# Four graph layers on one core: semaphores cleared inside stages, block-only preparations moved, two reloads split and one request moved

## The chip, the cores and the metric

The kernel runs on one core of a Trainium2 chip. The metric is the device time of one execution in microseconds (us); the median of three executions of the kernel before is 4069.77 us (4069.27 to 4072.3).

## The reference

A graph has 3125 nodes with 256 features and 50000 edges (`src`, `dst`, sorted by `dst`). Four layers follow one another, each added to its input and normalised over the features:

```python
# layer 0: one weight matrix per edge type (20), edges weighted
msg = h_all[edge_src, rel_type] * norm;  relu(segment_sum(msg, edge_dst))
# layer 1
relu(x @ W + segment_sum((x @ M)[edge_src], edge_dst))
# layer 2: attention with 4 heads, 4 node types, 8 edge types
k, q, v = _typed_matmul(h, ..., node_type)            # a matrix per node type
score = sum((q @ relation_att)[etype, col] * k[row]) * pri[etype] / 8
alpha = softmax of score over the edges of a target node
agg = segment_sum(alpha * (v @ relation_msg)[etype, row], col)
out = sigmoid(skip)[node_type] * _typed_matmul(agg, a_linears, node_type)
# layer 3: two graph convolutions
x = relu(segment_sum(norm * (x @ W[l])[src], dst) + b[l] + x_res @ resW + resb)
```

## The kernel before, in words

Nodes are held as 25 tiles of 128 rows (`NT`). The edges are sorted on the chip and held as 391 tiles of 128 edges (`USED`; 196 pairs). The program is a row of stages, each an `nc.Block()` with one instruction stream per engine; at a block's end all five engines meet in a barrier before the next block starts. In order:

1. `constants`, and `sort_and_relation_table` (L221 to L508): TensorE multiplies the nodes with the 20 matrices of layer 0 while VectorE sorts the edges and GpSimd (POOL) scatters the edges' records, 8 numbers each, to HBM (`records`, L313).
2. `reload_records` (L519): SyncE (SP) requests all sorted records back in one transfer (L529), clears the semaphores of the stages before (L530), VectorE and ScalarE turn two fields of every record into integer row numbers (`rows_i`, L540 and L546).
3. `aggregate_edges` for layer 0 (called `rel`), `first_layer_nodes` (L1696), `aggregate_edges` for layer 1 (`conv_edges`).
4. A block in which SP does nothing but clear spent semaphores (L2380).
5. `attention_tables` (L1835): the nodes are normalised, scattered by node type to `sorted_x` (L1902), read back in five parts of five tiles (L1889), multiplied by type, and the products scattered to `table8k`, `table8v` and `q_rows` (L1909, L1914). When all of these have landed, SP requests `q` back (L1895).
6. `attention_edges` (L1462): `attention_scores`, then `attention_sum`, in one block.
7. A second block that only clears (L2390), and a block in which VectorE adds two bias rows (L2399).
8. `attention_output` (L2109): SP loads weights, `skip` and the node types (L2148 to L2153); ScalarE waits for the last three before anything else (L2189); VectorE makes the gates from them; TensorE multiplies.
9. `aggregate_edges` (`gcn0_edges`), a third block that only clears (L2405), `hidden_nodes` (L1761), `aggregate_edges` again, `last_nodes`.

An edge sweep (`aggregate_edges`, and each half of `attention_edges`) works so: POOL issues one indirect gather per edge tile, 391 in all, into a ring of 16 pairs of tiles (`gather_all`, L624); SP relays arrivals to the others and hands slots back (`relay_pairs`, L641); for each of 220 items TensorE multiplies one-hot matrices with a gathered pair and VectorE adds the product to the window of its target nodes (L1062). POOL first needs a slot back at its 33rd gather. There are six sweeps, so 2346 gathers. The orders are written out by hand; nothing schedules them.

In the first sweep `ItemColumns` (L680) first makes the items' columns from the records: TensorE turns the records (L697), VectorE makes `tile_key` (L727) and `pick` (L731). In the scores TensorE waits for `q_back` before its first product (L1134), and ScalarE requests spread rows on its own DMA queue (L676).

## Time and profile before

| | us |
|---|---|
| median of three executions (lowest, highest) | 4069.77 (4069.27, 4072.3) |
| the profiled execution | 4077.45 |
| its span, from the first to the last instruction | 4075.5 |

| stage | from | to |
|---|---|---|
| sort and relation table | 0 | 559.8 |
| reload of the records | 559.8 | 568.3 |
| sweep `rel` | 568.3 | 1064.2 |
| first layer's nodes | 1064.2 | 1104.7 |
| sweep `conv_edges` | 1104.7 | 1600.3 |
| block that clears | 1600.3 | 1604.4 |
| attention tables | 1604.4 | 1873.0 |
| scores and sums | 1878.8 | 2890.3 |
| two blocks: clearing, biases | 2890.3 | 2896.5 |
| attention output | 2896.5 | 3002.8 |
| sweep `gcn0_edges` | 3002.8 | 3497.6 |
| block that clears | 3497.6 | 3500.7 |
| hidden nodes | 3500.7 | 3531 |
| sweep `gcn1_edges`, last nodes | 3531 | 4075.5 |

A timeline row reads: start, duration, engine, source line, operation, written tile <- read tiles, and in brackets how long the engine had been idle before and what ended that. "PEq", "POOLq", "SPq" are the sequencers of these engines; a release by one of them at the line of a block is the barrier. "DMA a<-b" is the landing of that transfer. SPq rows of DMA show the issuing instruction, not the transfer. Clearing a semaphore leaves no row.

### The profile page before, as it was taken

The numbers are of one execution on the slowest core, as the hardware profiler recorded it, in microseconds if no ns is written. First come the engines' busy times: TensorE is split into PE (matmuls) and PEld (weight loads), VectorE is DVE, ScalarE is ACT, GpSimd is POOL, SyncE is SP. The second block draws the span as 40 slices with busy tenths as digits, with TensorE's granted clock in tenths as the row PEclk, the third lists the DMA queues.
The fourth block names the chain that finished last, engine by engine and source line by source line (L and its number), as shares of the span: only waits on it lengthen the run. The fifth ranks groups of instructions, "written<-read, shape, count | busy, mean of one in ns | idle before, by whom it ended". The sixth has DMA issues, their size and how long they took to land. (4 is left out here: it accounts for less than half of the span.)

```text
span 4075.5 us, 64605 instructions
## 1 busy us (share of the span) xinstructions
PE 3135.5 (77%) x11818; PEld 2154.4 (53%) x11818; DVE 2219.7 (54%) x7526; ACT 926.8 (23%) x2670; POOL 2753.2 (68%) x2879
## 2 busy tenths in 40 slices
PE   6999938878788775795888878888877667677777
PEld 4444426656566653343667667676434444544444
DVE  6500037666666655445888858676654344334435
ACT  2333300000200001441444456555310000200001
POOL 4777767777677776335777767777237777477773
PEclk9999968898898986898887769777887888878788
DMA  4333323333333334677555546555223333333332
GB/s 146 149 146 150 145 76 106 105 105 106 96 106 105 106 105 140 244 299 243 164 165 163 163 138 176 161 163 160 66 74 106 105 105 106 99 105 106 106 105 85
DMA packets 226899, 540.02 MB, mean 133 GB/s; under 512 B 73483, under 2 KB 107949, under 8 KB 212877
## 3 DMA queue, kind: packets, MB, share of 16 engines
q0 software_dynamic: 136528, 374.97, 31.1%
q1 hardware_dynamic: 57880, 103.46, 7.0%
q10 hardware_dynamic: 32164, 57.91, 4.7%
q8 instruction: 123, 2.02, 0.2%
q14 instruction: 204, 1.66, 0.1%
HBM read 390.04 MB, written 146.09 MB: 132 GB/s over the span
## 5 line engine op out<-in xcount | busy, mean ns | idle before, releaser
L635 POOL DMA_INDIRECT gcn_edges_g<-table,rows_i x782 | 741.9, 949 | 397.9 <-issue 186.8
L1016 PE MATMUL ps<-gcn_edges_g,gcn_edges_onehot 128*128 x1760 | 618.8, 490 | 311.3 <-SPq L651 278.1
L1062 DVE TENSOR_TENSOR acc<-acc,ps 128x256 f32 (+1 forms) x880 | 370.2, 421 | 849.3 <-PE ps L1016 835.4
L1016 PEld LDWEIGHTS ps<-gcn_edges_g,gcn_edges_onehot 128*128 128x128 f32 x1760 | 382.7, 237 | 525.9 <-issue 477.3
L313 POOL DMA_INDIRECT records<-rec,slots x391 | 381.5, 976 | 167.6 <-issue 124.5
L635 POOL DMA_INDIRECT score_g<-table8v,rows_i x391 | 379.9, 972 | 132.6 <-issue 112.8
L635 POOL DMA_INDIRECT rel_g<-table,rows_i x391 | 372.1, 952 | 132.2 <-issue 96.0
L635 POOL DMA_INDIRECT score_g<-table8k,rows_i x391 | 373.1, 954 | 128.7 <-issue 110.7
L635 POOL DMA_INDIRECT conv_edges_g<-table,rows_i x391 | 371.8, 951 | 127.4 <-issue 93.3
L365 PE MATMUL ps<-w,xt 128*128 128x512 f32 x1000 | 435.8, 595 | 18.0 <-ACT xt L335 18.0
L1141 PE MATMUL ps<-q,onehot_t 128*128 x880 | 310.5, 486 | 120.4 <-DVE onehot_t L1240 96.1
L1375 PE MATMUL ps<-vx,score_onehot 128*128 128x260 f32 x880 | 303.5, 477 | 87.0 <-ACT vx L1399 48.9
L1016 PE MATMUL ps<-conv_edges_g,conv_edges_onehot 128*128 x880 | 277.8, 445 | 103.7 <-SPq L651 96.5
L1016 PE MATMUL ps<-rel_g,rel_onehot 128*128 x880 | 276.3, 443 | 96.1 <-SPq L651 88.8
L365 PEld LDWEIGHTS ps<-w,xt 128*128 128x128 f32 x1000 | 187.9, 190 | 251.2 <-issue 227.0
L1141 PEld LDWEIGHTS ps<-q,onehot_t 128*128 128x128 f32 x880 | 188.0, 236 | 161.8 <-issue 140.5
L1399 ACT ACTIVATE vx<-score_g,vx 128x64 f32 x880 | 234.5, 336 | 104.7 <-SPq L651 72.9
L1016 PEld LDWEIGHTS ps<-conv_edges_g,conv_edges_onehot 128*128 128x128 f32 x880 | 171.1, 215 | 162.7 <-issue 143.5
L1375 PEld LDWEIGHTS ps<-vx,score_onehot 128*128 128x128 f32 x880 | 182.6, 230 | 118.8 <-issue 95.7
L1016 PEld LDWEIGHTS ps<-rel_g,rel_onehot 128*128 128x128 f32 x880 | 172.2, 217 | 136.9 <-issue 118.0
L1054 DVE TENSOR_SCALAR gcn_edges_onehot<-cols,near 128x128 f32<-128x128 f32 x880 | 223.7, 308 | 1.3 <-issue 1.1
L343 ACT ACTIVATE tb<-ps 128x512 f32<-128x512 f32 x250 | 149.3, 597 | 296.4 <-PE ps L365 296.4
(327 smaller groups left out, 4799.4 us busy)
## 6 DMA issues: line engine op xcount, KB each, us to landing
table<-tb SPq DMA_DIRECT2D x50, 1280.0 KB, 4.6
score_dst_bc<-dst_rows ACTq DMA_DIRECT2D x110, 256.0 KB, 3.5
sum_dst_bc<-dst_rows ACTq DMA_DIRECT2D x110, 256.0 KB, 3.5
gcn_edges_g<-table,rows_i POOLq DMA_INDIRECT x782, 2.8
table<-acc SPq DMA_DIRECT2D x50, 128.0 KB, 1.7
records<-rec,slots POOLq DMA_INDIRECT x391
rel_g<-table,rows_i POOLq DMA_INDIRECT x391, 2.8
conv_edges_g<-table,rows_i POOLq DMA_INDIRECT x391, 2.7
```

The costliest lines, as they stand in the source:

```text
L313: pool.indirect_dma_start(out=m.records, out_offset=bass.IndirectOffsetOnAxis(ap=slots[:, j:j + 1], axis=0), in_=rec[:, j, :], in_offset=N ...
L343: nc.scalar.activation(tb[:, g // HG, (g % HG) * 512:(g % HG + 1) * 512], bank(m, g % 6, 0, 512), ACT.Copy).then_inc(emptied, 1)
L365: mm = pe.matmul(bank(m, g % 6, 0, 512), xt[:, k, :], w20[:, k, g * 512:(g + 1) * 512], start=(k == 0), stop=(k == 1))
L635: pool.indirect_dma_start(out=m.g[:, 2 * slot_of(p) + j, 0:D], out_offset=None, in_=table, in_offset=bass.IndirectOffsetOnAxis(ap=m.rows_i ...
L1016: mm = pe.matmul(bank(m, i % BANKS, 0, width), m.onehot[:, 2 * k + j, :], window(m.g, slot + j, 0, width), start=(j == 0), stop=(j == 1))
L1054: ins = nc.vector.tensor_scalar(m.onehot[:, 2 * k + j, :], m.cols[:, :], m.near[:, c:c + 1], None, ALU.is_equal)
L1062: nc.vector.tensor_tensor(acc, acc, bank(m, i % BANKS, 0, width), ALU.add).then_inc(added, 1)
L1141: mm = pe.matmul(bank(m, i % UNROLL, j * D, (j + 1) * D), onehot_t[:, i % 2, j * P:(j + 1) * P], q, start=True, stop=True)
L1375: mm = pe.matmul(bank(m, 4 + kk, 0, ACCW), m.onehot[:, 2 * kk + j, :], vx[:, kk, j, :], start=(j == 0), stop=(j == 1))
L1399: ins = nc.scalar.activation(vx[:, kk, j, h * DK:(h + 1) * DK], window(m.g, slot + j, h * DK, (h + 1) * DK), ACT.Copy, scale=vx[:, kk, j, ...
```

## The change

Clears. `take_spent` hands a list of spent semaphores over, and the next stage's SP clears them in its own block: 59 in `attention_tables` (after its small requests, before the wait for the scatters), 74 in `attention_output` (after the weights' requests, before the stores), 27 in `hidden_nodes` (before the stores). The three blocks that only cleared are gone.

Records. They come back in two transfers: tiles 0 to 31 (`FIRST`), then the rest, on a semaphore of its own (`rest_back`). The reload's block casts the first 32 tiles' row numbers only, on VectorE. The other casts, 360 and 392 columns, are VectorE's first work in `ItemColumns.vector`, behind a wait for `rest_back`; TensorE waits for it too. POOL waits for the casts (`rows_ready`) before its 33rd gather.

`q`. It is requested as SP's first instruction of `attention_edges`, not at the end of `attention_tables`.

Sorted rows. The five parts hold 2, 4, 5, 7 and 7 tiles where they held 5 each.

Biases and gates. The two additions of bias rows are VectorE's first work in the scores. `skip` is loaded in `attention_tables`; the gates compare `m.node_mark[:, :, 1]`, which the sort made, so the node types are not loaded again, and ScalarE's wait for the three small loads is gone.

```diff
@@ the reload and the first sweep @@
+FIRST = 32
 def clear_spent(sp, m):
-    for s in m.spent:
+    clear(sp, take_spent(m))
+def take_spent(m):
+    spent, m.spent = m.spent, []
+    return spent
+def clear(sp, spent):
+    for s in spent:
         sp.sem_clear(s)
...
-            sp.dma_start(m.rec[:, 0:USED, :], m.records.rearrange("(p t) f -> p t f", p=P)).then_inc(back, 16)
+            sp.dma_start(m.rec[:, 0:FIRST, :], sorted_records[:, 0:FIRST, :]).then_inc(back, 16)
+            sp.dma_start(m.rec[:, FIRST:USED, :], sorted_records[:, FIRST:USED, :]).then_inc(m.rest_back, 16)
             clear_spent(sp, m)
...
             dve.wait_ge(back, 16)
-            nc.vector.tensor_copy(m.rows_i[:, ROWS1, :], m.rec[:, :, F_SRC])
-        @block.scalar
-        def _(act):
-            act.wait_ge(blank, 2)
-            act.wait_ge(back, 16)
-            nc.scalar.activation(m.rows_i[:, ROWS20, :], m.rec[:, :, F_ROW20], ACT.Copy)
+            nc.vector.tensor_copy(m.rows_i[:, ROWS20, 0:FIRST], m.rec[:, 0:FIRST, F_ROW20])
@@ gather_all @@
     for p in range(PAIRS):
+        if rest_ready is not None and 2 * p == FIRST:
+            pool.wait_ge(rest_ready, 1)
@@ ItemColumns.tensor @@
+        pe.wait_ge(m.rest_back, 16)
@@ ItemColumns.vector @@
+        dve.wait_ge(m.rest_back, 16)
+        nc.vector.tensor_copy(m.rows_i[:, ROWS20, FIRST:TILES], m.rec[:, FIRST:TILES, F_ROW20]).then_inc(self.rows_ready, 1)
+        nc.vector.tensor_copy(m.rows_i[:, ROWS1, :], m.rec[:, :, F_SRC])
         nc.vector.tensor_scalar(m.tile_key[:, :], m.rec[:, :, F_DST], float(P), m.rowid[:, :], ALU.mult, ALU.add)
@@ attention_edges @@
         def _(sp):
+            sp.dma_start(m.q[:, 0:NT, :], m.q_rows[0:ROWS, :].rearrange("(t p) d -> p t d", p=P)).then_inc(m.q_back, 16)
             scores[0](sp)
...
         def _(dve):
+            for k in (0, 1):
+                nc.vector.tensor_tensor(m.bias[:, k, :], m.bias[:, k, :], m.bias[:, 2, :], ALU.add)
             scores[4](dve)
@@ hidden_nodes @@
+        old = take_spent(m)
...
         def _(sp):
+            clear(sp, old)
             for t in range(NT):
                 store_rows(sp, m, t, scaled, stored)
@@ attention_tables @@
+        old = take_spent(m)
...
-        PART = NT // 5
+        PARTS = ((0, 2), (2, 6), (6, 11), (11, 18), (18, NT))
...
+            sp.dma_start(m.skip[:, :], a.skip.rearrange("(o n) -> o n", o=1).to_broadcast([P, NTYPES])).then_inc(m.skip_in, 16)
+            clear(sp, old)
             sp.wait_ge(placed, 16 * NT)
-            for part in range(5):
-                sp.dma_start(xs[:, part * PART:(part + 1) * PART, :], m.sorted_x[part * PART * P:(part + 1) * PART * P, :]
+            for part, (lo, hi) in enumerate(PARTS):
+                sp.dma_start(xs[:, lo:hi, :], m.sorted_x[lo * P:hi * P, :]
                              .rearrange("(t p) d -> p t d", p=P)).then_inc(back[part], 16)
...
-            sp.dma_start(m.q[:, 0:NT, :], m.q_rows[0:ROWS, :].rearrange("(t p) d -> p t d", p=P)).then_inc(m.q_back, 16)
             sp.wait_ge(m.bias_in, 48)
+            sp.wait_ge(m.skip_in, 16)
...
             def pick(i):
                 if i < G:
-                    if i < NT and i % PART == 0:
-                        act.wait_ge(back[i // PART], 16)
+                    for part, (lo, hi) in enumerate(PARTS):
+                        if i == lo:
+                            act.wait_ge(back[part], 16)
@@ attention_output @@
+        old = take_spent(m)
...
-            sp.dma_start(skip[:, :], a.skip.rearrange("(o n) -> o n", o=1).to_broadcast([P, NTYPES])).then_inc(small_in, 16)
-            sp.wait_ge(types_zero, 1)
-            with nc.allow_non_contiguous_dma(reason="a node per partition"):
-                sp.dma_start(types_i[:, 0:NT - 1], a.node_type[0:(NT - 1) * P].rearrange("(t p) -> p t", p=P)).then_inc(small_in, 16)
-                sp.dma_start(types_i[0:LAST, NT - 1:NT], a.node_type[(NT - 1) * P:NODES].rearrange("(p o) -> p o", o=1)).then_inc(small_in, 16)
+            clear(sp, old)
             for t in range(NT):
                 store_rows(sp, m, t, scaled, stored)
...
-            act.wait_ge(small_in, 48)
             nc.scalar.activation(gate[:, :], skip[:, :], ACT.Exp, scale=-1.0).then_inc(exp_ready, 1)
...
-                ins = nc.vector.tensor_scalar(gates[:, ty, :], types_i[:, :], float(ty), skip[:, ty:ty + 1], ALU.is_equal, ALU.mult)
+                ins = nc.vector.tensor_scalar(gates[:, ty, :], m.node_mark[:, :, 1], float(ty), skip[:, ty:ty + 1], ALU.is_equal, ALU.mult)
@@ four_graph_layers: three blocks of this form are gone, and the block of the biases @@
-        with ExitStack() as c2:
-            block = c2.enter_context(nc.Block())
-            @block.sync
-            def _(sp):
-                clear_spent(sp, m)
```

How the instructions stand. SyncE around the reload, before (L515 ISA are the clears, the branches are the block's end and the next block's start) and in the changed kernel (clears: L527 ISA):

```order
L525 UNCONDITIONAL_BRANCH
L529 DMA rec_all<-records 128x3128
L515 ISA x29
L521 UNCONDITIONAL_BRANCH
L980 UNCONDITIONAL_BRANCH
```

```order
L537 UNCONDITIONAL_BRANCH
L539 DMA rec_all<-records 128x256
L540 DMA rec_all<-records 128x2872
L527 ISA x29
L532 UNCONDITIONAL_BRANCH
L991 UNCONDITIONAL_BRANCH
```

One transfer has become two, and the clears stand behind both. VectorE in the same place of the changed kernel: the cast of the reload, the block's end, and then the casts that stand ahead of `tile_key`:

```order
L551 CAST rows_i<-rec_all 128x32
L532 UNCONDITIONAL_BRANCH
L1042 UNCONDITIONAL_BRANCH
L736 CAST rows_i<-rec_all 128x360
L737 CAST rows_i<-rec_all 128x392
L738 TENSOR_SCALAR tile_key<-rec_all,rowid 128x392
```

SyncE from the read-back of the sorted rows to the scores' first relay, before and now:

```order
L1889 DMA xs<-sorted_x 128x5x256
L1889 DMA xs<-sorted_x 128x5x256 x4
L1895 DMA q<-q_rows 128x25x256
L1839 UNCONDITIONAL_BRANCH
L1473 UNCONDITIONAL_BRANCH
L645 TENSOR_LOAD release
```

```order
L1870 DMA skip<-in_skip 128x4
L527 ISA x59
L1874 DMA xs<-sorted_x 128x2x256
L1874 DMA xs<-sorted_x 128x4x256
L1874 DMA xs<-sorted_x 128x5x256
L1874 DMA xs<-sorted_x 128x7x256 x2
L1820 UNCONDITIONAL_BRANCH
L1484 UNCONDITIONAL_BRANCH
L1486 DMA q<-q_rows 128x25x256
L652 TENSOR_LOAD release
```

The request of `q` has moved across the barrier, and 59 clears stand ahead of the read-back.

## Rows read from the trace of the kernel before

**Rows 1.** Page: busy time, share of the span and instructions of each engine

```profile
PE 3135.5 (77%) x11818; PEld 2154.4 (53%) x11818; DVE 2219.7 (54%) x7526; ACT 926.8 (23%) x2670; POOL 2753.2 (68%) x2879
```

**Rows 2.** Timeline around the reload: start us, us, engine line operation, [idle before <-releaser]

```profile
559.84 0.33 SPq L529 DMA_DIRECT2D rec_all<-records  x1
566.38 0.52 DVE L540 CAST rows_i<-rec_all 128x392 int32<-128x392 f32 x1 [6.25 <-DMA rec_all<-records]
566.44 0.91 ACT L546 ACTIVATE rows_i<-rec_all 128x392 int32<-128x392 f32 x1 [51.65 <-DMA rec_all<-records]
568.28 0.98 POOL L635 DMA_INDIRECT rel_g<-table,rows_i  x1 [13.26 <-POOLq L521]
```

**Rows 3.** Timeline: first product and last gather of `rel`, one gather in the sums

```profile
592.95 1.64 PE L1016 MATMUL ps<-rel_g,rel_onehot 128*128 x3 [7.05 <-DVE rel_onehot L1051]
...
1058.36 0.95 POOL L635 DMA_INDIRECT rel_g<-table,rows_i  x1 [0.30 <-issue]
...
2425.01 0.95 POOL L635 DMA_INDIRECT score_g<-table8v,rows_i  x1 [13.69 <-SPq L647]
```

**Rows 4.** Timeline: from `rel` into the first node stage

```profile
1063.79 0.35 ACT L795 ACTIVATE dst_s<-ps 128x220 f32<-128x220 f32 x1
...
1064.45 0.43 DVE L1751 SCALAR_TENSOR_TENSOR acc<-acc,x 128x256 f32<-128x256 f32 x1 [0.94 <-PEq L964]
```

**Rows 5.** Timeline: from the second sweep into the tables

```profile
1599.90 0.42 DVE L1062 TENSOR_TENSOR acc<-acc,ps 128x257 f32 x1 [0.93 <-PE ps L1016]
...
1604.44 0.18 DVE L2065 TENSOR_SCALAR dis<-acc 128x25 f32<-128x25 f32 x1 [4.12 <-PEq L2380]
```

**Rows 6.** Timeline: the sorted rows come back; then two DMA issues with median landing

```profile
1642.05 4.23 SPq L1889 DMA_DIRECT2D xs<-sorted_x  x5
1646.76 0.72 ACT L2007 ACTIVATE xc<-xs 128x256 f32 x2 [10.68 <-DMA xs<-sorted_x]
...
xs<-sorted_x SPq DMA_DIRECT2D x5, 640.0 KB, 7.3
...
conv_w<-in_m SPq DMA_DIRECT2D x1, 256.0 KB, 3.0
```

**Rows 7.** Timeline: from the tables into the scores

```profile
1868.44 0.95 POOL L1914 DMA_INDIRECT table8v<-tb,into_i  x1 [2.79 <-DVE tb L2003]
1873.03 0.36 SPq L1895 DMA_DIRECT2D q<-q_rows  x1
...
1879.25 0.98 POOL L635 DMA_INDIRECT score_g<-table8k,rows_i  x1 [9.86 <-POOLq L1839]
...
1888.50 2.92 PE L1141 MATMUL ps<-q,onehot_t 128*128 x6 [22.92 <-DMA q<-q_rows]
```

**Rows 8.** Timeline: from the sums into the attention's output

```profile
2889.84 0.43 DVE L1448 TENSOR_TENSOR acc<-acc,ps 128x260 f32 x1 [1.59 <-PE ps L1375]
2895.05 0.88 DVE L2399 TENSOR_TENSOR bias<-bias 128x256 f32<-128x256 f32 x2 [4.79 <-PEq L2390]
...
2896.52 0.26 DVE L2215 TENSOR_SCALAR rden<-acc 128x100 f32<-128x100 f32 x1 [0.58 <-PEq L2262]
...
2898.19 1.09 PE L2167 MATMUL ps<-ident,acc 128*128 128x128 f32 x4 [8.50 <-DVE acc L2220]
...
2902.68 0.21 ACT L2190 ACTIVATE gate<-skip 128x4 f32<-128x4 f32 x1 [15.31 <-DMA types_i<-in_node_type]
...
2903.21 1.22 PE L2176 MATMUL ps<-q,xt 128*128 128x512 f32 x1 [3.93 <-ACT xt L2196]
```

**Rows 9.** Timeline: from the fifth sweep into the hidden nodes

```profile
3497.17 0.42 DVE L1062 TENSOR_TENSOR acc<-acc,ps 128x256 f32 x1 [1.61 <-PE ps L1016]
3500.69 1.40 PE L1662 MATMUL ps<-ident,acc 128*128 128x128 f32 x6 [3.67 <-PEq L2405]
```

**Rows 10.** Timeline: a gather beside a copy in the second sweep

```profile
1532.05 1.40 POOL L635 DMA_INDIRECT conv_edges_g<-table,rows_i  x1 [0.30 <-SPq L647]
1532.25 1.08 DVE L840 COPY near_rep<-near_s 128x1760 f32<-128x1760 f32 x1
```

More of the change, by code:

```diff
@@ L621, in free, with gather_all @@
                 self.eng.free_register(r)
-def gather_all(pool, m, table, rows, ahead_of=None):
+def gather_all(pool, m, table, rows, ahead_of=None, rest_ready=None):
     for p in range(PAIRS):
+        if rest_ready is not None and 2 * p == FIRST:
+            pool.wait_ge(rest_ready, 1)
         if p % 2 == 0:
@@ L977, in _ @@
         def _(pool):
-            gather_all(pool, m, table, rows)
+            gather_all(pool, m, table, rows, rest_ready=before.rows_ready if before else None)
         @block.sync
@@ L1498, in _ @@
         def _(dve):
+            for k in (0, 1):
+                nc.vector.tensor_tensor(m.bias[:, k, :], m.bias[:, k, :], m.bias[:, 2, :], ALU.add)
             scores[4](dve)
             sums[4](dve)
-def layer_norm(nc, m, stage, prepare, out):
-    with ExitStack() as ctx:
-        chain, stats_ready, root_ready = sems(ctx, nc, stage, "norm_chain", "norm_stats", "norm_root")
-        m.spent += [chain, stats_ready, root_ready]
-        block = ctx.enter_context(nc.Block())
-        @block.vector
-        def _(dve):
-            steps = [0]
-            def step(ins):
-                steps[0] += 1
-                ins.then_inc(chain, 1)
-                dve.wait_ge(chain, steps[0])
-            prepare(step)
-            for t in range(NT):
-                step_or_none = nc.vector.bn_stats(m.stats[:, t, :], m.acc[:, t, 0:D])
-            step(step_or_none)
-            for t in range(NT):
-                last = nc.vector.bn_aggr(m.mv[:, t, :], m.stats[:, t, :])
-            last.then_inc(stats_ready, 1)
-            dve.wait_ge(root_ready, 1)
-            step(nc.vector.reciprocal(m.rstd[:, :], m.std[:, :]))
-            for t in range(NT):
-                nc.vector.tensor_scalar(out[:, t, 0:D], m.acc[:, t, 0:D], m.mv[:, t, 0:1], m.rstd[:, t:t + 1],
-                                        ALU.subtract, ALU.mult)
-        @block.scalar
-        def _(act):
-            act.wait_ge(stats_ready, 1)
-            nc.scalar.activation(m.std[:, :], m.mv[:, :, 1], ACT.Sqrt, bias=m.eps[:, :], scale=1.0).then_inc(root_ready, 1)
 class TileNorm:
@@ L2129, in sb @@
             return ctx.enter_context(nc.sbuf_tensor(name, shape, dt))
+        old = take_spent(m)
+        skip = m.skip
         xt = sb("xt8", [P, 2, 2, P])
         rden = sb("rden", [P, NT, HEADS])
[L2133 to L2134 removed]
         gate = sb("gate", [P, NTYPES])
@@ L2137, in attention_output @@
         tmp = sb("tmp8", [P, 2, NTYPES - 1, D])
-        small_in, types_zero, chain, exp_ready, divided, turned, xt_ready, product, emptied, own, scaled, stored = sems(
-            ctx, nc, "out", "small_in", "types_zero", "chain", "exp_ready", "divided", "turned", "xt_ready",
+        chain, exp_ready, divided, turned, xt_ready, product, emptied, own, scaled, stored = sems(
+            ctx, nc, "out", "chain", "exp_ready", "divided", "turned", "xt_ready",
             "product", "emptied", "own", "scaled", "rows_stored")
-        m.spent += [small_in, types_zero, chain, exp_ready, divided, turned, xt_ready, product, emptied, own, scaled, stored]
+        m.spent += [chain, exp_ready, divided, turned, xt_ready, product, emptied, own, scaled, stored]
         norm = TileNorm(ctx, nc, m, "att")
@@ L2257, in _ @@
                 norm.norm(dve, i - 1, m.x)
-def vector_block(nc, m, stage, body):
-    with ExitStack() as ctx:
-        chain, = sems(ctx, nc, stage, "chain")
-        m.spent.append(chain)
-        block = ctx.enter_context(nc.Block())
-        @block.vector
-        def _(dve):
-            steps = [0]
-            def step(ins):
-                steps[0] += 1
-                ins.then_inc(chain, 1)
-                dve.wait_ge(chain, steps[0])
-            body(step)
 def four_graph_layers(nc, a, out):
@@ L2353, in four_graph_layers @@
         m.bias = sb("bias", [P, 3, D])
+        m.skip = sb("skip", [P, NTYPES])
         m.gathered = sems(ctx, nc, "all", *(f"gathered{k}" for k in range(SLOTS)))
         m.gather_stages = 0
-        m.mx_written, m.bias_in, m.gcn_w_in = sems(ctx, nc, "all", "mx_written", "bias_in", "gcn_w_in")
+        m.mx_written, m.bias_in, m.gcn_w_in, m.skip_in = sems(
+            ctx, nc, "all", "mx_written", "bias_in", "gcn_w_in", "skip_in")
         c5 = ctx.enter_context(ExitStack())
@@ L2389, in four_graph_layers @@
         attention_edges(nc, m, a)
-        with ExitStack() as c2:
-            block = c2.enter_context(nc.Block())
-            @block.sync
-            def _(sp):
-                clear_spent(sp, m)
-        def biases(step):
-            for k in (0, 1):
-                step(nc.vector.tensor_tensor(m.bias[:, k, :], m.bias[:, k, :], m.bias[:, 2, :], ALU.add))
-        vector_block(nc, m, "bias", biases)
         c5.close()
@@ L2404, in four_graph_layers @@
         aggregate_edges(nc, m, "gcn0_edges", m.table1, ROWS1, turned=(a.resw, m.bias[:, 0, :], m.x, ACT.Copy))
-        with ExitStack() as c2:
-            block = c2.enter_context(nc.Block())
-            @block.sync
-            def _(sp):
-                clear_spent(sp, m)
         h = sb("h", [P, NT, D])
```

22 lines of the change are left out of this document (8 added, 14 removed).

## The prediction, written before the changed kernel ran

> **What bounds the kernel now.** I read the page's busy times first. They show TensorE at 77% and POOL at 68% of the span [rows 1], and that is an average over fourteen stages, so it names no bound for any one of them. The chain of waits doesn't help: it names only the last stage's node work. So I went to the timelines around each place that the change touches, where the reader is to see who waits, for what, and how long.
>
> The sweeps come first, because two edits change when one starts. In `rel` POOL issues its first gather at 568.28 [rows 2] and its 391st at 1058.36 [rows 3]: 490.08/390 = 1.257 us per gather. One gather is busy 0.98 us and the next follows 0.30 us later "for nothing that the profile shows". POOL is never held up in `rel`. TensorE starts its products 24.7 us behind POOL (592.95) and ends with it. A sweep therefore ends a fixed time after POOL's first gather, however late the others begin, as long as their lag stays under the ring's 32 gathers, 32 × 1.257 = 40.2 us. Whatever lets POOL start earlier is passed on whole. Between stages everything is serial: a barrier waits for all, so what is removed there is passed on too.
>
> **The change part by part.** All times are of the profiled execution (4077.45 us, span 4075.5).
>
> *Barriers.* The step from `rel` into the nodes has a barrier and no clears: the last work ends at 1063.79 + 0.35 = 1064.14 and VectorE starts at 1064.45 [rows 4]. That is 0.31 us. Where a clearing block stands between, the gap is:
> - 57 clears: 1599.90 + 0.42 = 1600.32 to 1604.44, 4.12 us [rows 5];
> - 74 clears: 2889.84 + 0.43 = 2890.27 to VectorE's bias additions after 4.79 us idle [rows 6];
> - 27 clears: 3497.17 + 0.42 = 3497.59 to 3500.69, 3.10 us [rows 7].
>
> The slopes agree: (4.79 − 4.12)/17 = 0.039 and (4.12 − 3.10)/30 = 0.034 us per clear. The rest of each gap (about 2.1 us) is two barriers and something fixed of a block that holds only SP's work.
>
> *Clears moved into stages.* I leave one barrier of 0.31 in each gap: **−3.8** before the tables, **−2.8** before the hidden nodes; the one before the output is in the next item but one. The clears themselves are not gone. In the tables SP now does 59 (59 × 0.039 = 2.3 us) while it would only wait for scatters until 1642.05 [rows 8]; the output's 74 (2.9 us) and the hidden nodes' 27 (1.1 us) stand ahead of the first store, which waits for a finished tile and so for the stage's first products (TensorE's first is 6.7 us into the output stage). Cost nothing; without that cover it would be those 2.3, 2.9 and 1.1 us.
>
> *Records in two transfers.* Before: request at 559.84, VectorE released by the landing at 566.38, ScalarE's cast ends 566.44 + 0.91 = 567.35, POOL gathers at 568.28 [rows 2], so block's end to first gather is 0.93. Now POOL needs only a 128 KB transfer and a cast of 32 columns. The nearest transfer in the rows is a 256 KB one, 3.0 us from issue to landing (median of one) [rows 8]. I take 2.6 for half of it. The cast (392 columns take 0.52) is at most 0.15. That gives 559.84 + 2.6 + 0.15 + 0.93 = 563.5. SP's second request and 29 clears (1.1 us) end before this landing. So the first gather moves 568.28 → 563.5, **−4.8**. POOL's new wait at its 33rd gather comes 40.2 us later, when the casts are long done: nothing. TensorE and VectorE still need all records, so their start at 592.95 moves by at most 1 us and the lag grows from 24.7 to about 29 us, under 40.2.
>
> The unknown is how long SP itself holds the block open. `q` is requested at 1873.03, the block before ends with SP, and POOL's first gather comes at 1879.25 with 9.86 us idle, released by the barrier [rows 9]: (1879.25 − 0.93) − 1873.03 = 5.3 us pass between a large request and the block's end. If the records' second transfer holds SP as long (it is issued about 0.7 us after the first), the gather comes at 559.84 + 0.7 + 5.3 + 0.93 = 566.8 and the gain is only 1.5. The other end, a landing in 2.0 us, gives 5.4. I take 4.8 because the clears before were behind such a request too, and VectorE's release there was by the landing, but this row can't tell which ended last.
>
> *The two casts move beside gathers.* 360 and 392 columns, about 0.5 us each on VectorE. In the second sweep a copy of 1.08 us lay beside a gather, and that gather took 1.40 where its neighbours take 0.95 [rows 10]: 0.45 more. Two casts of together 1.0 us: **+0.4** (from 0 to 1.0, their whole duration). The Trainium skill, "SBUF — State Buffer", section "SBUF: two separate sides", has a trap for this: a VectorE copy of float32 from SBUF to SBUF locks GpSimd out, so that it can't write the descriptors of its DMA. By that rule POOL loses all of both casts, 1.0 and not 0.4, and the total below would be 27.0; here the values become integers, and the row supports a stretch of less than the copy's length.
>
> *Sorted rows in unequal parts.* Five requests from 1642.05 over 4.23 us, first use at 1646.76 after waiting for the landing: 4.7 us [rows 8]. The first part falls from 640 to 256 KB, and the 256 KB row says 3.0: **−1.6** (from 0, if the landing isn't set by size, to −2.6, if it came in 2.1). Later parts are larger but due later: the tables stage lasts over 220 us after that.
>
> *`q` requested in the scores.* The first gather of the scores follows the barrier. The last scatters are issued at 1868.44, SP sees them landed at 1873.03 [rows 9]. Without the 5.3 us of SP's request POOL starts at 1873.03 + 0.93 = 1873.96: **−5.3**. The transfer of `q` now runs beside gathers and the spread rows of ScalarE. TensorE waited for it 22.92 us and began at 1888.50. It is requested about 0.4 us later than before, and I allow 1.5 us more for the company: about 1890. TensorE's lag behind POOL's first gather grows from 9.3 to 16 us, less than the 24.7 that `rel` carries without a stall. The bias additions (0.88 us for both [rows 6]) lie under TensorE's wait.
>
> *Sums to output.* From 2890.27 to VectorE's 2896.52 [rows 6] are 6.25 us: clears, two additions, three barriers. One barrier of 0.31 stays: **−5.9**.
>
> *The gates.* In the output stage ScalarE waits 15.31 us for the node types and starts at 2902.68; TensorE's first product with weights is at 2903.21, 6.7 us after 2896.52, though its transposes ran at 2898.19 [rows 6]. Without that wait the product comes behind 1.67 us to the transposes, two of them (four take 1.09, so 0.55) and ScalarE's copy with its hand-over (about 0.6 by 2902.68 to 2903.21): 2.8 us after the start, **−3.9** (3 to 4.4). TensorE paces that stage afterwards, so it is passed on.
>
> | | us |
> |---|---|
> | conv → tables | −3.8 |
> | hidden nodes | −2.8 |
> | records (−4.8 + 0.4) | −4.4 |
> | sorted rows | −1.6 |
> | scores | −5.3 |
> | sums → output | −5.9 |
> | gates | −3.9 |
> | sum | **−27.7** |
>
> The profiled execution would come to 4049.8. It stands 7.7 us above the median of 4069.77; a difference carries over, so the median goes to **4042**.
>
> **The rivals.**
> - *B, SP holds the reload open.* The 5.3 us after `q` speak for it. Gain 1.5 in place of 4.8: 4045. Chance 0.12.
> - *C, `q` and the gathers hinder each other.* `q` is 3.1 MB on the same 16 engines as the gathers and the spreads. If it lands more than 20 us late, TensorE's lag passes 40.2 and POOL stalls; the scores' 5.3 are lost: 4047. For it: nothing in the rows; against it: 1.5 us expected against 24 us of slack. Chance 0.07. The Trainium skill, "DMA: Bandwidth & Descriptors", section "Issuing engines are not separate DMA queues", says that transfers of all issuers interleave on the same engines; by it the later landing is certain, and its size isn't given.
> - *F, the fixed part of a gap stays.* 3.10 = 2 × 0.31 + 27 × 0.039 + 1.4. If that 1.4 belongs to a sweep's end and not to the clearing block, three places keep it: +4.2, 4046. Against it: the end of `rel` shows only 0.31 [rows 4]. Chance 0.07.
> - *D, POOL doesn't set a sweep's end.* Then the earlier gathers of `rel` and the scores gain nothing (4.4 + 5.3 lost): 4052. Against it: TensorE waits for arrivals in the sweeps, and its lag at the start is caught up. In the scores it is weaker, since POOL idles 13.69 us at 2425.01 for a slot that the sums must have back [rows 3]. Chance 0.06.
> - *E, the other side: gathers become slower.* 2346 of them run one behind the other; code that sits elsewhere, or a semaphore more per wait, could change their pace. To turn 27.7 us of gain into 8.2 of loss needs (27.7 + 8.2)/2346 = 15 ns per gather, 1.2% of 1257: 4078. Nothing in the diff touches the loop but one wait. Chance 0.03, half of it strong enough for slower.
>
> **How the numbers follow.** A measurement of this kernel can tell about 0.2%, 8 us, from no change. The forecast has 0.65 and its own range 4036 to 4047 (records 1.5 to 5.4, sorted rows 0 to 2.6, casts 0 to 1, gates 3 to 4.4). B, C and F lie inside 4034 to 4050, which also allows two of them together with a little; D and E are outside. Faster by over 8 us needs under 4062, which all cases but E give; E's 0.03 and 0.01 for a loss I haven't named make same 0.02 and slower 0.02, so faster is 0.96.
>
> **What would show each step.** In the changed kernel: POOL's first gather about 3.7 us after SP's first records request (B: 7); about 0.3 us idle on VectorE at the start of the tables; the first copy of sorted rows 3.0 us after its request; POOL's first gather of the scores about 0.9 us after the tables' end, TensorE's first product near 16 us later and POOL without a stall in its next 60 gathers; about 0.3 us from the last sum to `rden`; the first weighted product 2.8 us after that; about 0.3 us before the hidden nodes; 1.257 us per gather in `rel`. The prediction is wrong if gaps of over 2 us stay at the three places where the clearing blocks stood, if `rel` lasts longer by what its gathers start earlier, or if the gathers' pace changes by more than 5 ns.

## The result, and the profile after

A remark for reading the prediction: four of its group numbers are off against the section of rows above. Where it writes [rows 6] read group 8 (sums to output), for [rows 7] group 9 (hidden nodes), for [rows 8] group 6 (sorted rows and landings) and for [rows 9] group 7 (tables to scores). From here on the numbers are those of the section.

| | before | changed |
|---|---|---|
| median of six executions, us | 4070.50 | 4048.26 |
| lowest and highest | 4067.2, 4075.22 | 4045.73, 4048.99 |
| the profiled execution's span | 4075.5 | 4046.6 |

The changed kernel takes 0.9944 of the time (95% interval 0.9934 to 0.9955), 22.2 us less. The forecast was 27.7 less, 4042 us, with a range of 4034 to 4050. By the interval the difference is 18 to 27 us, so the forecast difference itself lies just outside it. The two spans differ by 28.9, but the profiled execution of before was itself slow against its median. Of the 28.9, 8.0 us lie in stretches that the change does not touch: both halves of the attention's edges from first to last gather (2.9), the last stage (2.3), and three other sweeps (2.8). That leaves 20.9 for the change.

The page's busy line of the changed kernel, which answers to [rows 1]: the engines do the same work in less time.

```profile
PE 3128.9 (77%) x11818; PEld 2148.3 (53%) x11818; DVE 2219.3 (55%) x7527; ACT 925.4 (23%) x2669; POOL 2749.2 (68%) x2879
```

Timeline of the changed kernel around the reload (answers to [rows 2]):

```profile
560.06 0.33 SPq L539 DMA_DIRECT2D rec_all<-records  x1
...
560.43 0.43 SPq L540 DMA_DIRECT2D rec_all<-records  x1
562.17 0.19 DVE L551 CAST rows_i<-rec_all 128x32 int32<-128x32 f32 x1 [1.85 <-DMA rec_all<-records]
563.50 0.98 POOL L642 DMA_INDIRECT rel_g<-table,rows_i  x1 [8.26 <-POOLq L532]
...
567.23 0.51 DVE L736 CAST rows_i<-rec_all 128x360 int32<-128x360 f32 x1 [4.87 <-DMA rec_all<-records]
...
567.30 1.48 POOL L642 DMA_INDIRECT rel_g<-table,rows_i  x1 [0.31 <-issue]
567.65 0.52 DVE L737 CAST rows_i<-rec_all 128x392 int32<-128x392 f32 x1
568.08 0.58 DVE L738 TENSOR_SCALAR tile_key<-rec_all,rowid 128x392 f32<-128x392 f32 x1
```

The 128 KB land 2.1 us after their request (2.6 was the estimate), and the first gather comes 3.44 us after it, where it was 8.44. SP's second transfer holds nothing open. One gather, the one beside VectorE's casts, takes 1.48 instead of 0.95. Then the sorted rows (answers to [rows 6]) and the entry into the attention's output and the hidden nodes (to [rows 8] and [rows 9]), timelines of the changed kernel:

```profile
1632.90 2.88 SPq L1874 DMA_DIRECT2D xs<-sorted_x  x5
1635.74 0.72 ACT L1992 ACTIVATE xc<-xs 128x256 f32 x2 [8.82 <-DMA xs<-sorted_x]
...
2877.61 0.42 DVE L1459 TENSOR_TENSOR acc<-acc,ps 128x260 f32 x1 [1.62 <-PE ps L1386]
2878.33 0.20 ACT L2171 ACTIVATE gate<-skip 128x4 f32<-128x4 f32 x1 [3.20 <-PEq L1479]
2878.35 0.26 DVE L2194 TENSOR_SCALAR rden<-acc 128x100 f32<-128x100 f32 x1 [0.32 <-PEq L1479]
...
2880.91 3.68 PE L2158 MATMUL ps<-q,xt 128*128 128x512 f32 x4 [0.20 <-ACT xt L2177]
...
3474.37 0.42 DVE L1073 TENSOR_TENSOR acc<-acc,ps 128x256 f32 x1 [2.00 <-PE ps L1027]
...
3475.50 1.51 PE L1641 MATMUL ps<-ident,acc 128*128 128x128 f32 x6 [1.28 <-PEq L975]
```

First copy 2.84 us after the request; one barrier of 0.32 before `rden`; first weighted product 2.56 us after that; 0.71 from the last addition to the hidden nodes. All of this is close to the forecast. This is not, the timeline from the tables into the scores (answers to [rows 7]):

```profile
1859.00 0.95 POOL L1899 DMA_INDIRECT table8v<-tb,into_i  x1 [2.89 <-DVE tb L1988]
1869.15 0.36 SPq L1486 DMA_DIRECT2D q<-q_rows  x1
...
1869.81 0.99 POOL L642 DMA_INDIRECT score_g<-table8k,rows_i  x1 [9.86 <-POOLq L1820]
```

POOL idles 9.86 us between its last scatter and its first gather. It idled the same 9.86 us before [rows 7]. SP no longer requests anything there, and the gap has not moved by a hundredth. The instructions of the block's line say what holds it. First before, then the changed kernel (columns: line, engine, operation, count, duration in ns as least/median/most, first and last start):

```profile
L1839 ACTq DRAIN  x1: 1027/1027/1027, 1866.7 to 1866.7; - x1
...
L1839 POOLq DRAIN  x1: 10131/10131/10131, 1868.2 to 1868.2; - x1
...
L1839 SPq DRAIN  x1: 7/7/7, 1873.6 to 1873.6; - x1
```

```profile
L1820 ACTq DRAIN  x1: 607/607/607, 1857.7 to 1857.7; - x1
L1820 POOLq DRAIN  x1: 10119/10119/10119, 1858.8 to 1858.8; - x1
...
L1820 SPq DRAIN  x1: 7/7/7, 1863.8 to 1863.8; - x1
```

Every engine has a DRAIN at the line of the block, an instruction of its sequencer that stands ahead of the barrier. A sequencer may reach it while its engine is still busy: POOL's row starts at 1858.8, before the last scatter does, so its end is the number to read. SP's is over at 1863.8, when the scatters have landed. POOL's ends at 1858.8 + 10.1 = 1868.9, some 5 us after SP, and the barrier follows. Before, SP was ready at 1873.6, its request of `q` included, and POOL's DRAIN ended at 1878.3. In both kernels that end is 8.95 us past the end of POOL's last scatter.

### The profile page after: what moved, and what is told of

It reads as the page before. It is cut to its first block and busy times, and to the rows that moved or that the text cites. A ratio compares the mean times of both kernels' runs of the same rounds, so it can differ in the third digit from the quotient of the medians.

```text
span 4046.6 us, 64559 instructions
## 1 busy us (share of the span) xinstructions
PE 3128.9 (77%) x11818; PEld 2148.3 (53%) x11818; DVE 2219.3 (55%) x7527; ACT 925.4 (23%) x2669; POOL 2749.2 (68%) x2879
```

## The experiments

In each, "gap" is the time from the start of POOL's last table scatter to its first score gather: 10.81 in both kernels. The medians are given as differences from the kernel before on the same chip; such a difference is uncertain by up to 7 us, so two of them can't be told apart when they lie within some 8 us, and positions in the traces carry the verdicts. (The changed kernel's own difference is 22.2.)

**1. The request of `q` goes back.**

```diff
@@ attention_tables, after the waits for the scatters @@
+            sp.dma_start(m.q[:, 0:NT, :], m.q_rows[0:ROWS, :].rearrange("(t p) d -> p t d", p=P)).then_inc(m.q_back, 16)
@@ attention_edges @@
-            sp.dma_start(m.q[:, 0:NT, :], m.q_rows[0:ROWS, :].rearrange("(t p) d -> p t d", p=P)).then_inc(m.q_back, 16)
```

> Only the request of q goes back to where it stood, the end of the tables' block. Theory 1 (the barrier between tables and scores waits for POOL's own DRAIN, which ends 8.95 us after its last scatter, whatever SP does): POOL's first gather of the scores stays 10.8 us after the start of its last scatter, as in both kernels so far; the time is that of the changed kernel within 2 us; TensorE's first score product comes 3 to 5 us earlier after that gather than in the changed kernel. Theory 2 (the prediction's: SP's request held the block): the gap returns from about 5.5 to 10.8 us, so it would have had to be short in the changed kernel, and the time rises by 5.3 us.

Measured: 24.2 us under before, gap 10.81. Timeline of this kernel:

```profile
1858.39 0.95 POOL L1899 DMA_INDIRECT table8v<-tb,into_i  x1 [1.48 <-DVE tb L1988]
1863.23 0.36 SPq L1879 DMA_DIRECT2D q<-q_rows  x1
1869.20 0.99 POOL L642 DMA_INDIRECT score_g<-table8k,rows_i  x1 [9.86 <-POOLq L1819]
...
1878.38 2.07 PE L1152 MATMUL ps<-q,onehot_t 128*128 x4 [21.52 <-DMA q<-q_rows]
```

SP's request lies wholly inside POOL's DRAIN. Moving it across the barrier gains nothing, and in the changed kernel TensorE's first product comes 19.7 us after POOL's first gather where it comes 9.2 after it here (I expected a difference of 3 to 5). Theory 1 holds. The DMA views of the three kernels show the landing of `q` after its request, in order before, this one, changed:

```profile
q<-q_rows SPq DMA_DIRECT2D x1, 3200.0 KB, 15.1
```

```profile
q<-q_rows SPq DMA_DIRECT2D x1, 3200.0 KB, 14.8
```

```profile
q<-q_rows SPq DMA_DIRECT2D x1, 3200.0 KB, 20.0
```

In the company of gathers and spread rows it lands 5 us later; I had allowed 1.5 and 0.4 for the later request. The ring absorbs it: POOL's 391 score gathers take 490.1 us in the changed kernel and 489.3 here.

**2. POOL waits for the landings first.**

```diff
@@ attention_tables, end of POOL's part @@
+            pool.wait_ge(stored[0], 16 * G)
+            pool.wait_ge(stored[1], 16 * G)
```

> POOL waits at the end of the tables' block until all table scatters have landed, and only then reaches the block's end. The landing is seen 4.6 us after the last scatter's start. Theory 1a (the DRAIN starts when POOL gets there and takes about 8.9 us of its own): first gather 10.8 + 3.6 = 14 us or more after the last scatter, time up by 3 to 4 us. Theory 1b (the DRAIN waits for something that runs from the scatter on, and is over 8.95 us after it in any case): the gap stays 10.8 and the time the same. Theory 1c (the DRAIN waits only for landings it has not seen, so that none is left): the gap falls to about 6 us and the time by 5.

Measured: 21.2 us under before; gap 14.66, timeline of this kernel:

```profile
1857.65 0.95 POOL L1899 DMA_INDIRECT table8v<-tb,into_i  x1 [2.91 <-DVE tb L1990]
1872.31 0.98 POOL L642 DMA_INDIRECT score_g<-table8k,rows_i  x1 [13.71 <-POOLq L1820]
```

The rows of SP and POOL at the block's line, as above:

```profile
L1820 SPq DRAIN  x1: 7/7/7, 1862.4 to 1862.4; - x1
L1820 POOLq DRAIN  x1: 8946/8946/8946, 1862.5 to 1862.5; - x1
```

All data had landed by 1862.5, and still 9.8 us pass to the first gather. So the DRAIN does not wait for the table scatters' data; it takes 8.95 us of its own from when POOL gets there (1a).

**3. The small scatter last.** For the last group `q_rows` (1 KB rows) is scattered after the tables (8 KB rows).

```diff
@@ attention_tables, POOL, in the loop over groups; q_scatter() is the scatter as it was @@
...
+                if i < G - 1:
+                    q_scatter()
...
+                if i == G - 1:
+                    q_scatter()
```

> For the last group of rows alone POOL issues the small scatter of q's rows (1 KB a row) after the two scatters of the tables (8 KB a row), not before them. Theory A (the DRAIN's length goes with the size of what was issued last: 4.5 us after a gather or scatter of 1 KB rows at the ends of the sweeps and the sort, 8.95 us after the 8 KB one): the DRAIN ends 4.5 us after the q scatter, so about 1.26 + 0.95 + 4.5 + 0.9 = 7.6 us from the table scatter's start to the first gather in place of 10.8; time down by 3. Theory B (it goes with everything still under way): no shorter than 10.8, and up to 1.3 longer; time the same or up by 1.

Measured: 22.7 us under before. POOL idles once more 9.86 us between its last scatter (1858.50, now `q_rows`) and its first gather (1869.33). Whether the last is a scatter of 8 KB rows or of 1 KB rows, the DRAIN ends 8.95 us past it; theory A falls, and the gap is at the upper end of theory B: 12.08 us from the table scatter.

**4. Each moved clear three times.**

```diff
-def clear(sp, spent):
+def clear(sp, spent, times=1):
-    for s in spent:
+    for s in spent * times:
@@ the three stages @@
-            clear(sp, old)
+            clear(sp, old, 3)
```

> Every one of the 59, 74 and 27 moved clears is done three times over. Theory (clears inside the stages lie under other work): time the same within 1 us; 118, 148 and 54 more clears of 0.039 us are 4.6, 5.8 and 2.1 us of SP's time, before the scatters have landed and before the first stores. Rival (they sit on the path, since the stores or the read-back of the sorted rows wait behind them): up by as much as 12.5 us in all, seen at the sorted rows' request, or at the stages' ends.

Measured: 20.1 us under before. The sorted rows are requested 2.43 us after their last scatter (2.42 in the changed kernel). From `rden` to the first gather of the next sweep it takes 102.3 us (changed: 102.6), from the hidden nodes' first product to their sweep's 31.4 (changed: 32.5). No place of the clears grew; the clears are hidden. That the median lies 2 us above the changed kernel's is inside the uncertainty.

**5. One reload.**

```diff
-            sp.dma_start(m.rec[:, 0:FIRST, :], sorted_records[:, 0:FIRST, :]).then_inc(back, 16)
-            sp.dma_start(m.rec[:, FIRST:USED, :], sorted_records[:, FIRST:USED, :]).then_inc(m.rest_back, 16)
+            sp.dma_start(m.rec[:, 0:USED, :], m.records.rearrange("(p t) f -> p t f", p=P)).then_inc(back, 16)
...
-            nc.vector.tensor_copy(m.rows_i[:, ROWS20, 0:FIRST], m.rec[:, 0:FIRST, F_ROW20])
+            nc.vector.tensor_copy(m.rows_i[:, ROWS1, :], m.rec[:, :, F_SRC])
...
+            nc.scalar.activation(m.rows_i[:, ROWS20, :], m.rec[:, :, F_ROW20], ACT.Copy)
```

> Only the records' split is undone: one transfer, and both casts in the reload's block. Theory (POOL paces the sweep, so its start is passed on): first gather of rel 8.4 to 8.5 us after the block's first instruction in place of 3.4; last gather later by 4.6 (5.0, less 0.4 that the casts cost beside gathers), end of rel later by as much; time up by 4.6. Rival D of the prediction (the sweep's end does not hang on POOL's first gather): the end of rel moves by less than 1 us.

Measured: 20.2 us under before. First gather 8.67 us after the request, last gather 498.85 after it; in the changed kernel 3.44 and 493.90. So the first gather comes 5.2 us later, the last one 4.95, and the next stage starts 5.0 later against the request (504.6, 499.7). All but 0.3 of POOL's start is passed on; rival D is out. The cast's cost of 0.4 can't be told from the sweep's length: first to last gather takes 489.5 to 490.5 us in the kernels with split records on this clock, and 490.1 and 490.2 in the two without. The median moved by 2 us where 4.6 were expected, which its uncertainty allows.

**6. Equal parts.** `PARTS = ((0, 5), (5, 10), (10, 15), (15, 20), (20, NT))` in place of the unequal ones.

> Only the sorted rows' parts are made equal again (5 tiles each). Theory (the first part's landing is passed through the tables' stage): the first copy of sorted rows comes 4.7 us after the request in place of 2.84, and the last table scatter, and the time, 1.9 us later. Rival (the gain is given back inside the stage, where POOL's scatters wait for earlier scatters to land; in the changed kernel the first copy was 11.02 us earlier than before and the last table scatter only 9.44): the last scatter moves by 0.3 us or so.

Measured: 23.7 us under before. Timeline of this kernel:

```profile
1632.89 4.04 SPq L1874 DMA_DIRECT2D xs<-sorted_x  x5
1637.58 0.72 ACT L1992 ACTIVATE xc<-xs 128x256 f32 x2 [10.67 <-DMA xs<-sorted_x]
```

4.69 us to the first copy, and 203.3 from the request to the last of the 28 (changed: 201.4, before: 203.3). The 1.9 us pass through the stage's pipeline to its last copy, and the last `table8v` scatter is 2.0 later against the request (228.1, 226.1). The median shows none of it (1.5 under the changed kernel's), within its uncertainty. What follows the last copy differs: from the last `q_rows` scatter to the last `table8k` scatter it takes 3.7 us in before and in runs 5 and 7, and 5.1 to 5.2 in the changed kernel and in runs 1, 2, 4, 6 and 8 (run 3 issues them in another order). This run has equal parts and 5.07, run 7 has unequal ones and 3.74, so the parts don't set it. The giving-back that the rival read from two profiles is that difference; its cause stays open, and with it whether these 1.4 us belong to the change.

**7. The clearing blocks return.**

```diff
@@ four_graph_layers, ahead of the tables, the output, the hidden nodes @@
+        with ExitStack() as c2:
+            block = c2.enter_context(nc.Block())
+            @block.sync
+            def _(sp):
+                clear_spent(sp, m)
```

> The three blocks that only clear come back, ahead of the tables, the output and the hidden nodes; the bias additions stay inside the scores. Theory (a block costs its clears and two barriers): up by 3.4 before the tables (4.1 against 0.75), by 4.5 before the output and by 2.4 before the hidden nodes, 10.3 us in all. Rival (what the blocks took is only the POOL DRAIN that a stage's end shows anyway): each gap grows by the clears alone, 2.3 + 2.9 + 1.1 = 6.3 us.

Measured: 14.4 us under before, so 7.8 above the changed kernel. Timelines of this kernel at the three places:

```profile
1596.74 0.18 DVE L2051 TENSOR_SCALAR dis<-acc 128x25 f32<-128x25 f32 x1 [4.59 <-PEq L2337]
...
2881.21 0.26 DVE L2194 TENSOR_SCALAR rden<-acc 128x100 f32<-128x100 f32 x1 [4.79 <-PEq L2347]
...
3481.09 1.30 PE L1641 MATMUL ps<-ident,acc 128*128 128x128 f32 x5 [3.50 <-PEq L2359]
```

The gaps are 4.60, 4.79 and 2.93 us where the changed kernel has 0.80, 0.32 and 0.71. That is 10.5 us, as the theory has it (10.3); the clears alone would be 6.3, so a block costs 1.2 to 1.6 us beside its clears. The biases' block, the last 1.5 us of the sums' gap of 6.25, is in none of the runs.

**8. The node types waited for.**

```diff
@@ attention_output @@
+                sp.dma_start(types_i[:, 0:NT - 1], a.node_type[0:(NT - 1) * P].rearrange("(t p) -> p t", p=P)).then_inc(small_in, 16)
+                sp.dma_start(types_i[0:LAST, NT - 1:NT], a.node_type[(NT - 1) * P:NODES].rearrange("(p o) -> p o", o=1)).then_inc(small_in, 16)
...
+            act.wait_ge(small_in, 32)
             nc.scalar.activation(gate[:, :], skip[:, :], ACT.Exp, scale=-1.0).then_inc(exp_ready, 1)
...
-                ins = nc.vector.tensor_scalar(gates[:, ty, :], m.node_mark[:, :, 1], float(ty), skip[:, ty:ty + 1], ALU.is_equal, ALU.mult)
+                ins = nc.vector.tensor_scalar(gates[:, ty, :], types_i[:, :], float(ty), skip[:, ty:ty + 1], ALU.is_equal, ALU.mult)
```

> Only the node types' loads and ScalarE's wait for them come back in the attention's output. Theory (TensorE paces that stage, so its first product passes through): first weighted product 6.2 to 6.7 us after the stage's start in place of about 2.5, the end of the stage and the time 4.3 us later. Rival (the stage's end is set by its stores and absorbs it): the end moves by less than 1 us.

Measured: 18.7 us under before. First weighted product 6.1 us after `rden` (changed: 2.56), the next sweep's first gather 107.3 after it (changed: 102.6, before: 106.9). The product is 3.5 us later and the next sweep 4.7, so nothing is absorbed; where the further 1.1 us come from is open.

**9 to 11. Extra DRAINs.** These three ran on a chip on which every kernel is slower (before 5357.76 us; mean granted clock 0.74 against 0.86), so they are compared with each other alone. POOL's DRAIN of the tables takes 10.13 us on it too (run 11), 8.95 past the last scatter.

```diff
@@ attention_tables, POOL, after the table scatters of group i @@
+                if i < G - 1:
+                    pool.drain()
```

That is run 9. Run 10 has `if i == G // 2:` in that place, and run 11 is the changed kernel unedited.

> POOL also executes a DRAIN of its own after every group of three scatters in the tables' stage (27 of them), where it idles some 3 us anyway. The block's DRAIN has now ended 8.95 us after POOL's last scatter in five kernels, also when it came after the landing and when a small scatter was last; it ended 4.55 us after the last of 391 gathers and 2.2 us after the last of 25 two-number scatters. Theory D1 (a DRAIN works off something that the scatters since the last DRAIN left behind): the last one takes 1 to 3 us, the gap from the last table scatter to the first gather falls from 10.8 to 4 to 6 us (then SP's wait for the landing, 4.6 us after the scatter, may end last), and the time by 5; each of the 27 takes 3 us or less and hides in the idle time. Theory D2 (a DRAIN has a fixed length in this block): the gap stays 10.8, and 27 DRAINs of up to 9 us make the stage far longer, up to 27 x 5 us.

> One extra DRAIN alone, after the group in the middle of the tables' stage. D1 with a cost for each scatter: it and the last DRAIN share the length, each some 4 to 6 us, the gap falls to 6.5 to 8. D1 with a cap (only what the last few dozen left counts): both take 8.95 us, the gap stays 10.8. D2: the same as with a cap; the 8.95 us in the middle delay the stage by 0 to 6 us.

> The changed kernel unedited, on the same chip as the two kernels with extra DRAINs, so that they can be compared with it: 22 us less than before, the gap from the last table scatter to the first gather 10.8 us.

Measured: 5385.60, 5341.77 (a single execution) and 5335.30 us. The changed kernel is 22.5 us under before here too (14 to 32 by the interval). The last rows of POOL in the tables' stage, with DRAINs between (run 9), with one (run 10), without (run 11):

```profile
2606.58 0.95 POOL L1899 DMA_INDIRECT table8v<-tb,into_i  x1 [0.30 <-issue]
2613.69 0.99 POOL L642 DMA_INDIRECT score_g<-table8k,rows_i  x1 [6.16 <-POOLq L1820]
```

```profile
2553.93 0.95 POOL L1899 DMA_INDIRECT table8v<-tb,into_i  x1 [1.47 <-DVE tb L1990]
2561.27 0.99 POOL L642 DMA_INDIRECT score_g<-table8k,rows_i  x1 [6.38 <-POOLq L1820]
```

```profile
2547.03 0.95 POOL L1899 DMA_INDIRECT table8v<-tb,into_i  x1 [2.50 <-DVE tb L1988]
2557.85 0.99 POOL L642 DMA_INDIRECT score_g<-table8k,rows_i  x1 [9.86 <-POOLq L1820]
```

The gap falls from 10.8 to 7.3 with one earlier DRAIN and to 7.1 with 27. So the length isn't fixed by the block, and D2 falls. The extra DRAINs' own rows, run 9 and then run 10, here with the scatter before it:

```profile
L1903 POOLq DRAIN  x27: 6267/7818/9545, 2349.9 to 2595.5; - x27
```

```profile
2449.20 0.95 POOL L1899 DMA_INDIRECT table8v<-tb,into_i  x1 [1.03 <-DVE tb L1990]
...
L1903 POOLq DRAIN  x1: 8342/8342/8342, 2449.0 to 2449.0; - x1
```

The end of a DRAIN, counted from the end of the last table scatter before it, goes up with the number of scatters since the DRAIN before: in run 9 mostly 5.2 us after 3 scatters (5.1 to 6.9) and 5.5 after 28, in run 10 5.5 after 39 and 7.2 after 70, in run 11 8.95 after 109. D1 is right that a DRAIN works off something that scatters leave, and its gap for run 10 (6.5 to 8) came true. It is wrong that two DRAINs share the length, for 7.2 and 5.5 add up to 12.7 and not to 8.95, and that three scatters leave 1 to 3 us: some 5 us come with any DRAIN behind a table scatter. They don't hide in POOL's idle time either, since its next scatters wait; run 9 takes 50 us more than run 11. In run 9 SP is as late as POOL at the end (its DRAIN row stands at 2612.8, POOL's ends at 2612.7).

**12. No DRAIN of POOL.** Blocks can be opened so that POOL ends without one.

```diff
-        block = ctx.enter_context(nc.Block())
+        block = ctx.enter_context(nc.Block(no_gpsimd_drain=True))
```

So in every block.

> The changed kernel with every block told not to end POOL with a DRAIN (the barrier then takes POOL as it arrives; SP still waits for the landings). Theory (POOL's DRAIN is what held the barrier from the tables to the scores, and the sort's end): the barrier comes with SP's sight of the landing. Last table scatter to the scores' first gather: 4.6 + 0.3 + 0.66 = 5.6 us in place of 10.8. Last record scatter to the request of the records: 2.6 us in place of 5.8. Sweep's last addition to the next stage about 0.32 us at all places, in place of 0.3 to 0.8. Together some 9 to 10 us less than the changed kernel, about 31 us less than before. Rival (the work of the DRAIN is only put off, and POOL's next gather waits for it): the barrier comes earlier but POOL's first gather stays 10.8 us behind the last scatter, and the time stays within 2 us of the changed kernel, but for the sort's 3 us.

Measured: 4042.52 us against 4072.91, 0.9923 of before (0.9910 to 0.9937), 30.4 us less. Timeline of this kernel at the two places:

```profile
554.41 0.96 POOL L314 DMA_INDIRECT records<-rec,slots  x1 [0.30 <-issue]
557.05 0.32 SPq L539 DMA_DIRECT2D rec_all<-records  x1
...
1856.86 0.95 POOL L1899 DMA_INDIRECT table8v<-tb,into_i  x1 [3.37 <-DVE tb L1988]
1861.93 0.36 SPq L1486 DMA_DIRECT2D q<-q_rows  x1
...
1862.59 0.98 POOL L642 DMA_INDIRECT score_g<-table8k,rows_i  x1 [4.79 <-POOLq L1820]
```

The gap is 5.73 instead of 10.81, and the records are requested 2.64 us after their last scatter instead of 5.77. From the last addition of a sweep to the tables and to the hidden nodes it takes 0.39 (changed: 0.80, 0.71). The work of the DRAIN is not merely put off: the 391 score gathers take 489.8 us (changed: 490.1). The two places give 8.2 us. By the medians against before this kernel is 8.2 us faster than the changed one too, but that difference is uncertain by some 7 us, so the close agreement is chance.

## Why the prediction was right, and where it was wrong

| term | forecast | in the traces |
|---|---|---|
| first gather of `rel` | −4.8 | −5.0 |
| casts beside gathers | +0.4 | +0.5 |
| conv → tables | −3.8 | −3.3 |
| sorted rows | −1.6 | −1.9 |
| `q`, start of the scores | −5.3 | 0.0 |
| sums → output | −5.9 | −5.9 |
| gates | −3.9 | −4.3 |
| hidden nodes | −2.8 | −2.4 |
| sum | −27.7 | −22.3 |

The table covers the places that the forecast named. It leaves out the 1.4 us lost at the end of the tables (run 6); with them the traces give 20.9, which is also what the spans leave for the change. The measured difference of 22.2, between 18 and 27, agrees with either. Seven of the eight terms are right to 0.5 us.

The time lay inside the stated range, 4034 to 4050, and the forecast's own range, 4036 to 4047, missed it by 1 us. (That range doesn't follow from its terms: their bounds added up give 4040 to 4048.5.) That the stated range held is luck: it was wide enough for rivals B, C and F, and what happened is none of them, though it cost the 5.3 us of rival C.

What failed is one step, "without the 5.3 us of SP's request POOL starts at 1873.96". The prediction took the last event that a timeline shows ahead of the barrier for its cause. A row of the block's own line, POOL's DRAIN of 10.1 us from 1868.2, stood in the same trace and ended last. The request of `q` held SP for 0.6 us (1873.03 to 1873.6), not for 5.3, and all of it lay beside that DRAIN, so the term is 0.0. Runs 1 to 3 and 12 show it. The same confusion gave rival B its price: its 5.3 us after a large request were POOL's DRAIN as well. In the reload POOL issues nothing, its DRAIN there takes 0.04 us, and the block ended right after the cast.

- *Barriers and clears.* One barrier is 0.32 before the output but 0.80 and 0.71 at two sweeps' ends, since POOL's DRAIN after the last gather ends there 0.4 to 0.5 us after VectorE's last addition. Without that DRAIN both are 0.39 (run 12). Rival F (1.4 us at each place) was wrong in size, but 0.4 to 0.5 us of it is real at two places. Clears are free where they were put (run 4); with their blocks they cost 10.5 us (run 7).
- *Records.* Passed on but for 0.3 us (run 5); rival D is out.
- *Casts.* The gather beside the two casts lost 0.53 us, but not in proportion to them, as the prediction had reckoned from a copy. What repeats is the distance of its end from VectorE's. It ends at 568.78, 0.12 us after VectorE's `tile_key`, which follows the casts (568.08 + 0.58). In runs 3, 6 and 7 it is 0.12 after `tile_key` too, and in runs 1 and 4 0.12 to 0.13 after the second cast, where the loss is 0.14 and 0.20. The copy of [rows 10] ends at 1532.25 + 1.08 = 1533.33 and its gather at 1533.45, again 0.12 later. Where a gather starts while the copy already runs, it ends 0.82 after it. Timeline of the changed kernel:

```profile
1527.31 1.08 DVE L851 COPY near_rep<-near_s 128x1760 f32<-128x1760 f32 x1
1527.52 1.69 POOL L642 DMA_INDIRECT conv_edges_g<-table,rows_i  x1 [0.30 <-issue]
```

  So these gathers look as if they wait for VectorE's instruction to end, and the loss goes by how the two fall together. By the rule of the Trainium skill, "SBUF — State Buffer", section "SBUF: two separate sides" with its part "A bandwidth-pool intuition that's wrong", a copy of float32 within SBUF keeps GpSimd from writing its descriptors until VectorE has ended and about 115 ns more; the 0.12 us agree with it. The prediction had two readings wrong here: the rule doesn't make POOL lose the whole length of the casts, and [rows 10] don't speak against the rule. No run changes this overlap alone.
- *Sorted rows, gates.* Both passed through their stages (runs 6 and 8). That TensorE paces the output stage was the argument; the runs show the passing on, not its cause.
- *`q` beside gathers.* Rival C's later landing is there: 20.0 us against 14.8, which agrees with the Trainium skill, "DMA: Bandwidth & Descriptors", section "Issuing engines are not separate DMA queues". Its consequence is not: TensorE's lag of 19.7 us is under the ring's 40, and POOL does not stall.
- *Rival E.* In `rel` the pace is 490.5/390 = 1.258 us per gather against 1.257.

## What to carry to other kernels

When a wait ends with a barrier, list every engine's own rows at the block's line before naming what held it; the last transfer seen ahead of a barrier may lie under another engine's DRAIN. Removing work from one engine ahead of a barrier is worth only as much as that engine ended after the next latest. A stage's clears, loads and small arithmetic are free inside a neighbouring stage on an engine that waits, while a block for them alone costs its work and 1.2 to 1.6 us more (run 7). Here SP's own waits cover the landings, and leaving POOL's DRAINs out gained another 8.2 us at two places (run 12).

## What the hardware showed that was not expected

POOL's DRAIN at the end of a block takes time of its own. In the tables it ended 8.95 us past the last of 109 scatters, and it took 8.95 when it began after all had landed (run 2). It ended 4.55 past the last of 391 record scatters of 8 numbers each (10.9 to 11.6 on the chip of runs 9 to 11), mostly 4.55 past the last of 391 or 782 gathers of 1 KB rows (up to 5.3, in `gcn0_edges` of the changed kernel), and 2.2 past the last of 25 scatters of two numbers. Within the tables its length goes up with the number of scatters since the last DRAIN, from 5.2 for 3 to 8.95 for 109 (runs 9 to 11). What sets it is not settled by these: not the size of the last transfer (run 3), and not the count alone, since 782 took less than 109. Nothing was seen to need it here: without it (run 12) the time fell.
